# Graph attention on one core: the P·V products of two graphs are issued ahead of the scores of their slot

## The reference

```
h = jnp.maximum(_layernorm(x, axis=-1), 0.0)
q = _split_heads(h @ Wq + bq); k = ... Wk, bk; v = ... Wv, bv
scores = jnp.einsum('bhqd,bhkd->bhqk', q, k) / jnp.sqrt(jnp.asarray(HD, input_graph.dtype))
scores = scores + beta * adj_e
scores = jnp.where(adj_e > 0, scores, jnp.asarray(-9000000000000000.0, scores.dtype))
probs = jax.nn.softmax(scores, axis=-1)
out = jnp.einsum('bhqk,bhkd->bhqd', probs, v)
x = x + out
```

## Time and profile before

| | us |
|---|---|
| median of three runs | 500.69 |
| lowest, highest | 500.36, 500.71 |
| the profiled execution | 500.28 |
| its span, first to last instruction | 498.5 |
| PE, ACT, DVE busy in it | 487.5, 455.3, 429.3 |

### The profile page before, as it was taken

The page is one execution under the profiler, slowest core; times in us unless marked ns, Lnnn a source line. Parts: engine busy times, 40 slices in busy tenths (PEclk is TensorE's granted clock), DMA queues, the critical chain, the costliest instruction groups (busy, mean ns, idle before and its releaser), DMA issues.

```text
span 498.5 us, 17211 instructions
## 1 busy us (share of the span) xinstructions
PE 487.5 (98%) x5112; PEld 413.1 (83%) x5112; DVE 429.3 (86%) x2243; ACT 455.3 (91%) x1841; POOL 181.2 (36%) x272
## 2 busy tenths in 40 slices
PE   8999999999999999999999999999999999999996
PEld 7787888888888888888888888888888888888874
DVE  6689898899898898899888889889889888765896
ACT  3789999999999999999989999998999999999895
POOL 5621234334434424433433443333443333331143
PEclk9999999999999999999999999999999999999999
DMA  7556787777878777777776878777786766454432
GB/s 241 197 173 192 230 243 248 226 238 226 269 226 258 244 219 236 246 256 236 246 233 216 259 237 247 254 225 238 228 263 220 237 219 188 137 178 158 159 114 80
DMA packets 114844, 108.90 MB, mean 218 GB/s; under 512 B 12784, under 2 KB 99696, under 8 KB 114800
## 3 DMA queue, kind: packets, MB, share of 16 engines
q1 hardware_dynamic: 114800, 108.45, 69.5%
HBM read 57.28 MB, written 51.12 MB: 217 GB/s over the span
## 4 chain that ended last, share of the span: by engine, by line
PE 91%; DVE 4%; issue 1%; ACT 1%; POOL 0%; DVEq 0%; ACTq 0%
PE G_ps L1084 41%; PE S_ps L1155 20%; PE S_ps L1101 10%; PE PT_ps L1139 10%; PE PT_ps L1123 9%; DVE probs L900 1%; DVE probsT L934 1%; DVE h_lo L846 1%; ACT h_hi L739 0%; PE G_ps L1139 0%; ACT w_hi L647 0%; PE G_ps L1170 0%; DVE w_raw L956 0%; PE S_ps L1164 0%; POOL w_lo L589 0%
## 5 line engine op out<-in xcount | busy, mean ns | idle before, releaser
L667 ACT ACTIVATE probs<-probs,negmax 128x128 f32<-128x128 f32 x528 | 204.7, 397 | 1.7 <-DVE rinv L890 1.7
L900 DVE CUSTOM_DVE_ANT_0 probs<-S_ps,bias 128x128 f32<-128x128 f32 x768 | 167.0, 286 | 45.0 <-PE S_ps L1101 44.0
L1084 PE MATMUL G_ps<-h_hi,w_hi 128*128 128x512 f32 x288 | 120.4, 419 | 1.2 <-ACT qk L712 0.9
L1084 PE MATMUL G_ps<-h_hi,w_lo 128*128 128x512 f32 x288 | 116.1, 404 | 0.0
L1084 PE MATMUL G_ps<-h_lo,w_hi 128*128 128x512 f32 x288 | 113.1, 394 | 0.0
L688 ACT ACTIVATE probs_blocks<-probs,negmax 128x128 f32<-128x128 f32 x240 | 93.5, 391 | 16.4 <-DVE negmax L900 15.8
L667 ACT ACTIVATION_READ_ACCUMULATOR probs<-probs,negmax 128x1 f32 x528 | 103.5, 196 | 0.0
L574 POOL TENSOR_TENSOR var_eps<-meanvar,eps_col 128x1 f32<-128x1 f32 x64 | 18.0, 282 | 225.2 <-DVE meanvar L823 224.9
L601 POOL TENSOR_TENSOR w_raw<-w_raw,rinv 128x384 f32<-128x384 f32 x60 | 56.5, 941 | 57.8 <-issue 54.1
L622 POOL TENSOR_TENSOR w_raw<-w_raw,x_ring 128x384 f32<-128x384 f32 x63 | 64.6, 1025 | 19.5 <-POOL w_raw L601 6.4
L1101 PEld LDWEIGHTS S_ps<-qk 32*128 32x128 f32 x1536 | 48.8, 185 | 21.4 <-issue 21.1
(11 more groups left out here) (73 smaller groups left out, 741.3 us busy)
## 6 DMA issues: line engine op xcount, KB each, us to landing
probs_rows<-probs_blocks SPq DMA_DIRECT2D x60, 256.0 KB, 2.2
probs_moved<-probs_rows SPq DMA_DIRECT2D x240, 64.0 KB, 2.5
out_dram<-w_raw SPq DMA_DIRECT2D x63, 192.0 KB, 2.2
x_ring<-in_x_dram SPq DMA_DIRECT2D x62, 192.0 KB, 2.9
w_raw<-out_rows SPq DMA_DIRECT2D x120, 96.0 KB, 2.4
xhat_rows<-xhat_blocks SPq DMA_DIRECT2D x28, 384.0 KB, 3.6
xhat_moved<-xhat_rows SPq DMA_DIRECT2D x112, 96.0 KB, 2.4
out_rows<-xhat SPq DMA_DIRECT2D x15, 384.0 KB, 2.3
```

What stands on the lines that cost most here:

```text
L667: last = nc.scalar.activation(p, p, ACT.Exp, bias=negmax[:, e, j * KC + m:j * KC + m + 1], scale=TURN, accum_out=rowsum[:, e, m * HC + j:m ...
L900: return nc.vector.tensor_tensor_reduce(probs[:, a, j, m, :], S_ps[:, j, m * N:(m + 1) * N], bias[(z.par + 1) % 2][:, z.s, :], 1.0, LARGES ...
L1084: mm = nc.tensor.matmul(G_ps[:, u % 2, :], pairs[n][0], pairs[n][1], start=(n == 0), stop=(n == len(pairs) - 1))
```

## The change

In the regular slots the products P·V now stand ahead of the scores on PE. The rest concerns the start and the end: the ACT casts of the value weights are divided otherwise over the first slots (one rather than three in slot s = 1, three rather than one in s = 2), one low part goes from DVE to POOL, `add_bv` of graph 1 stands right behind its masks, the reciprocals of the last four graphs stand ahead of the masks, and in `last_probs` the last quotient and the transposes for it stand earlier.

```diff
+                self.early_v = self.static and n == 1 and s < 2
...
-                parts = [KC + z.s] * (z.static and z.groups(0) == 0 and z.s < GROUP - 1)
+                parts = [KC + z.s if z.s < GROUP - 1 else 2 * KC + 1] * (z.static and z.groups(0) == 0)
...
-                    for _ in range((2, 3, 1)[z.s]):
+                    for _ in range((2, 1, 3)[z.s]):
                         weights_high()
...
                     reciprocals(z)
                     store_probsT(z, 1)
+                    quotient(z)
                     dve.wait_ge(third_pv, 1)
                     nc.vector.tensor_copy(outT_end[:, 0:N], outT_last(0)).then_inc(third_outT[0], 1)
-                    quotient(z)
                     return
-                if z.O and not z.F:
+                if z.O:
                     reciprocals(z)
                 if z.A:
                     mask(z)
                 for d in z.pv:
                     store_outT(z, d)
+                if z.early_v and not z.first_a:
+                    add_bv(z)
...
                 if z.F and z.A:
-                    reciprocals(z)
                     add_bv(z)
...
                     weights_low(2 * KC)
-                    weights_low(2 * KC + 1)
-                values_here = z.A and z.P and not z.closing and not z.first_a
+                values_here = z.A and z.P and not z.closing and not z.early_v
...
                 if z.static and z.a == 0:
-                    pe.wait_ge(w_lo_dve, 1 + KC)
+                    pe.wait_ge(w_lo_dve, KC)
+                    pe.wait_ge(w_lo_pool, 2 * KC)
...
                 transpose_last_two(z, 0)
+                transpose_out(z)
+                transpose_last_two(z, 1)
                 pe.wait_ge(v_stored, z.e + 1)
                 pe.wait_ge(pT_stored[0], z.e + 1)
                 third_times_v(0, range(HC)).then_inc(third_pv, 1)
-                transpose_last_two(z, 1)
-                transpose_out(z)
...
+                for d in z.pv:
+                    probs_times_v(z, d)
                 if z.A:
                     scores(z)
-                for d in z.pv:
-                    probs_times_v(z, d)
```

## The result

The changed kernel takes 532.8 us, the median of six runs (531.06 to 533.54). The kernel before, run beside it, takes 500.5 (500.36 to 500.71). The ratio is 1.064, with an interval from 1.063 to 1.065: it is slower by 6.4%. The profiled execution of after took 532.77 us, with a span of 530.9; that of before 500.28 and 498.5. So 32.5 us have to be found.

The account below looks back on a forecast made before the run. PE's stream was taken as the bound, busy 487.5 of 498.5 us, with DVE's cushions deciding the loss. 11.2 + 16.3 + 2.1 = 29.6 us on 500.28 gives 529.9, plus 0.41 for the median: 530.3, range 525 to 538.

Parts of the forecast that it names:

- The exchange on PE: PE's passages between tile forms in odd slots: three changes stay three, cost 0, bounds 0.1 us either way per slot.
- Slots with s = 1: PE's transposes wait for DVE's later readings of the products: +0.8 us in each of 14 slots, 11.2 together.
- Slots with s = 3: The next scores on PE wait for DVE's later stored values: +1.25 us in each of 13 slots, 16.3 together.
- Graph 3: First odd slot: products now open it and wait for ACT's copies, 0.85 us, plus 1.25 for the values: +2.1.
- Nothing for that either: DMA round trip of the probabilities: data 1.45 us later, read in a slot 0.8 or 1.25 later; cost 0.
- ACT's copies: ACT's copies ahead of odd slots' products come 1.45 us later but in time: 0, at most 2.8 us in all.
- rival (c): Products open odd slots too early for ACT's copies: 0.4 us more in each of 28 slots, 541.5 us; chance 0.1.
- Start and end: Moved casts, early values and reciprocals: 0 in sum; bounds -0.9 and +0.3 for the casts, 1 either way at the end.
- Rival (a): PE's stream counts and its order is free: 500.7 us or slightly less; chances 0.03 faster, 0.02 the same.
- the cushions of 0.85 and 0.24 us: Time between DVE's stored values and PE's next scores before the change: 0.85 us with s = 1, 0.24 with s = 3.
- Rival (b): Only the values hold PE up, not the transposes: 14 x 0.75 instead of 14 x 0.8, 529.6 us; no chance of its own.
- The forecast of 16.0 us from graph 30's scores to graph 32's: Sign on PE's timeline: this stretch takes 16.0 us rather than 14.77.

Follow-up runs that it names:

- the first experiment: The kernel before with only the products and the scores exchanged in PE's order, all other edits left out: 532.8 us, ratio 1.064.
- the one cure: The changed kernel with SP issuing the probabilities' reads ahead of the normalised rows' write and first read of outputs in s = 2 slots: 528.8 us, ratio 1.056.
- the kernel with both cures: The changed kernel with DVE reading the products ahead of the masks in odd slots, and SP issuing the probabilities' reads first in s = 2 slots: 516.4 us, ratio 1.032.

## Why the prediction was right, and where its sum was not

I forecast 530.3 us, slower, from 525 to 538. It is 532.8. The mechanism is the one forecast, and of its terms the largest hold:

- **The exchange on PE, 0.** Right. A passage from column to row tiles shows no price: the products take 257.54 - 256.09 = 1.45 us, and the scores 258.42 - 257.54 = 0.88, which are the figures of the earlier trace rows in the other order. The kernel with projections ahead fits, since it loses its time without that passage. A fourth passage does have a price: with one product ahead, slots with s = 1 lose 0.16 us though PE waits for nothing there. The drains at each change of mode that the Trainium skill tells of ("TensorEngine Tiling (Array Packing)", Key Properties) are three in either order, and the equal figures agree with that.
- **Slots with s = 1, 14 x 0.8 = 11.2.** Right: each loses 0.80 us, and it is the reading of the products that the transposes wait for (0.54 in graph 29's slot), with the values just behind, as the step had it. The delay grows by 10.65 rather than 11.2 because the s = 0 slots ahead of them give back 0.6, for which I had no term; 0.45 of it falls in those of graphs 8, 12 and 48, where in the kernel before PE waits for a stretched low part (last section).
- **Slots with s = 3, 13 x 1.25 = 16.3.** The size of one is right to the hundredth, the count is not. (The 0.25 us for the signal I had read where the profile marks no wait, so it was only an upper bound; measured where PE does wait, it is 0.24.) In the slots of graphs 51 and 55 DVE has less to do (in graph 51's its statistics of 0.55 us, L820, are missing, in graph 55's its normalisation too, since no group is left to prepare); they lose 0.74 and 0.35. The term is 14.8.
- **Graph 3, 2.1.** Measured 2.08.
- **"Nothing for that either", for the DMA round trip of the probabilities.** This is the step that failed. I set 1.45 us of lateness of the data against slots that start 0.8 or 1.25 later, and concluded that the difference was small. It is 0.67, the 2.13 - 1.46 of SP's timelines above, and I never looked at what was left between landing and reading before: DVE waits there for 0.6 us in the whole program before, but it was close behind. Nor did I see that SP issues the reads behind five others, which puts them 3.4 us behind their write in either kernel. The term measures 4.0 us, twice: as what the groups take above their share (in slots with s = 2), and as what the kernel with the reads ahead wins back.
- **ACT's copies, 0, and rival (c).** In the changed kernel the count holds; the line of waits for the copies is not among those that matter. But I gave the rival a chance of 0.1 as an alternative, when it is a third bound lying close beneath: with DVE and DMA out of the way it shows, 14 times, 4.6 us.
- **Start and end, 0.** Alone they are nothing: 500.6 against 500.5. In place they are +0.60 at the start, +0.9 at the hand-over and -0.6 at the end. POOL did take the gain of the casts, as the prediction had it, for its low part is what PE waits for now:

```profile
23.16 0.50 PE L1085 MATMUL G_ps<-h_hi,w_hi 128*128 128x512 f32 x1 [0.78 <-POOL w_lo L590]
```

  Of the 0.60, 0.3 is there at graph 0's scores already; the early values add the other 0.3 net (0.66 won up to graph 2's scores, 0.96 lost behind them) instead of nothing. The hand-over I had not taken up by itself. It is ACT's copy, late in the last odd slot, for which PE waits once:

```profile
501.88 0.63 PE L1140 MATMUL G_ps<-ident,probs 128*128 128x128 f32 x4 [1.21 <-ACT probsT L698]
```

- **Rival (a)**, that only the order in PE's stream changes and the time stays, is excluded by the first experiment. What it had for it, PE at 98%, was no evidence: the cushions of 0.85 and 0.24 us behind that figure decided. The Trainium skill ("Perfetto Trace Analysis", Identifying the Most-Contended Engine) calls the engine with the highest occupancy the most contended, but for TensorE it has the busy share of the weight loads, or the share of peak arithmetic, taken in place of the matmuls' busy time. The prediction left that exception out: by it PE stands at 83% here, below ACT's 91%. Neither share tells what this change costs.
- **Rival (b)**, only the values, falls: the transposes wait for the reading 14 times in every kernel in which the scores of slots with s = 1 come 1.3 us later or more and DVE reads the products behind the masks, that with projections ahead included; with one product ahead they don't wait.

The forecast of 16.0 us from graph 30's scores to graph 32's is met by 280.61 - 264.39 = 16.22; the 0.20 above it is the DMA's, in the even slot. With every term at its measured size the sum is 0.6 + 2.1 + 10.7 + 14.8 + 4.0 + 0.9 - 0.6 = 32.5, of which 27.6 (the terms of s = 1, s = 3 and graph 3, forecast at 29.6) were foreseen. The whole is only 2.9 us above the sum forecast, and errors of opposite sign help in that: 2.0 us too much in these terms, 4.9 too little for the DMA, the start, the hand-over and the end together.

What stays open: why two slots early in the program, those of graphs 10 and 14, lose 1.5 and 0.7 us to the DMA and others 0.0 to 0.5; the time from issue to landing varies from 1.8 to 4.0 us, and no experiment changed that alone. Of the 5.2 us that DVE is less busy after, 2.6 are the low part (`h_lo`, 581 ns on average before, 535 after: it is never stretched there) and 1.2 the low parts of the weights, of which one went to POOL; the rest is open.

## What to carry to other kernels

Where one engine's stream is meshed with another's, an exchange of two blocks can cost the engine that runs them nothing, as here, and still shift the whole of the partner's slot by the block that now goes first. What decides is then not how busy an engine is but the cushion between each result of the partner and its reader; list these cushions, take the shift off each, and sum over the slots those that turn negative. Do the same for every round trip by DMA, with the place of its issue in its queue: that was the list that I left one item short. And to change one engine's order means to change that of its partners too, and the bounds below may still come up one after the other: here the one cure gave 4 us, both gave 16, and 16 remained. And a wait in the list is not yet a cost: the 7.6 us that DVE waits for the DMA with s = 1 alone cost PE nothing.

## What the runs showed that I had not expected

**DVE's low part doubles beside POOL's quotient.** In the kernel with both cures the low part `h_lo` (two operands from SBUF, 128x384) takes 1.07 us in most slots with s = 0. All engines at the start of such a slot (start, us, engine, line; order of the answer):

```profile
270.10 0.95 PE L1108 MATMUL S_ps<-qk 32*128 32x128 f32 x24 [0.27 <-DVE v L932]
270.11 0.83 POOL L605 TENSOR_TENSOR w_raw<-w_raw,rinv 128x384 f32<-128x384 f32 x1
...
270.29 1.07 DVE L850 SCALAR_TENSOR_TENSOR h_lo<-hT,h_hi 128x384 fp32r<-128x384 f32 x1 [0.44 <-ACT h_hi L743]
...
271.41 0.51 PE L1091 MATMUL G_ps<-h_hi,w_hi 128*128 128x512 f32 x1 [0.37 <-DVE h_lo L850]
```

Elsewhere it takes 0.52 to 0.58 us (0.55 at graph 31's end). Here it starts 0.18 us behind POOL's quotient and ends at 271.36, 0.42 behind the quotient's end at 270.94: nearly as if it had begun when POOL was done. It is so in 11 of its 56 in this kernel, in none of 56 in the changed kernel, in 4 of 56 in the kernel before, there too each time 0.06 to 0.23 us behind the same step of POOL, and in 11 of 56 in that with the exchange in slots with s = 1 alone. From the kernel before:

```profile
83.08 0.83 POOL L601 TENSOR_TENSOR w_raw<-w_raw,rinv 128x384 f32<-128x384 f32 x1
83.14 1.18 DVE L846 SCALAR_TENSOR_TENSOR h_lo<-hT,h_hi 128x384 fp32r<-128x384 f32 x1
```

The Trainium skill ("SBUF — State Buffer", SBUF: two separate sides) says that VectorE and GpSimd have a pair of ports between them, that whichever starts first holds it for its whole instruction, and that a VectorE operation with two inputs from SBUF takes part in that. The traces agree, in both directions. In the 13 kernels 54 low parts start within 0.3 us behind a quotient. Of these, 51 take 0.98 to 1.24 us instead of 0.55 and end 0.41 to 0.42 behind the quotient's end, wherever in it they started. The other three start within 0.05 behind it, and there it is the quotient that takes 1.24 to 1.26 us instead of 0.83. So it does, with 1.23 to 1.25, all 28 times that it starts within 0.02 us behind a low part, which then keeps its 0.56. So moving DVE by some tenths of a us, without any change to its work, can cost PE time: in the kernel with both cures PE's matmuls wait for the low part 10 times, 0.28 to 0.42 us each. No experiment moved POOL's quotient itself.

**The DMA wait doesn't scale with the shift.** Half the shift of the scores leaves it at 7.9 us, the whole has 9.2 in the kernel with the exchange alone and 7.9 in the changed one, and the exchange in slots with s = 1 alone has 7.6. Each figure is of one execution, and the kernel with the end edits alone, with no exchange, has 3.4 against the 0.6 of the kernel before, so differences of 1 or 2 us say little. What does differ is what PE pays: 5.2 us in slots with s = 2 for the 9.2, about 4 for either 7.9, and nothing for the 7.6. In the first three the products open the slots with s = 3 and wait for the late probabilities; in the last they stand behind the scores there, which leaves them 0.88 us more. That this is the reason is my reading; why the wait itself is as long as it is, no run has tested.
